# History encoder for 512 users: adding the mask term to the scores and laying out the weight sums on GpSimd, and keeping the short-term sum in PSUM

## What is computed

```python
decay = jnp.exp(-alpha * hist_age_hours) * maskf
mean_hist = (hist_items * maskf[..., None]).sum(1) / (maskf.sum(1, keepdims=True) + 1e-06)
q = mean_hist @ Wq.T
k = jnp.einsum('btd,ed->bte', hist_items, Wk)
v = jnp.einsum('btd,ed->bte', hist_items, Wv)
scores = jnp.einsum('bd,btd->bt', q, k) * scale + jnp.log(decay + 1e-12)
scores = jnp.where(hist_mask, scores, -jnp.inf)
attn = jax.nn.softmax(scores, axis=-1)
long_term = jnp.einsum('bt,btd->bd', attn, v)
# lk marks the last 5 positions below the user's count of unmasked items
short_term = (hist_items * lk[..., None]).sum(1) / denom
g = jax.nn.sigmoid(ctx @ gate_w.T + gate_b)      # ctx: mean popularity, mean age of those 5
user = g * short_term + (1.0 - g) * long_term
# then a layer norm over the 128 columns
```

## Time and profile before

| | us |
|---|---|
| runs without profile | 206.36, 208.58, 211.24 (median 208.58) |
| the profiled execution | 206.09 |
| its span, first to last instruction | 204.4 |
| TensorE busy | 168.8 (83%) |
| VectorE busy | 174.1 (85%) |
| GpSimd busy | 143.0 (70%) |
| ScalarE busy | 118.8 (58%) |

### The profile page before, as it was taken

One profiled execution on the slowest core, in us unless ns is written; L12 is line 12 of the kernel. 1 busy time (PEld: TensorE's weight loads), 2 busy tenths in 40 slices (PEclk: granted clock), 3 DMA queues, 4 the chain that ended last, 5 costly groups with the idle time before them and its releaser, 6 DMA issues.

```text
span 204.4 us, 6882 instructions
## 1 busy us (share of the span) xinstructions
PE 168.8 (83%) x2005; PEld 102.9 (50%) x2005; DVE 174.1 (85%) x1332; ACT 118.8 (58%) x646; POOL 143.0 (70%) x167
## 2 busy tenths in 40 slices
PE   0172864887999699899999999999999999997890
PEld 0132432444565456565655565656565656564570
DVE  0513989989999999999899999898999998989703
ACT  2002255587767377667676777676677776768410
POOL 3467982488959587777869887769698877486311
PEclk9998555699999999999999999999999999999998
DMA  7949969996888878988988899988888998600000
GB/s 36 303 153 304 257 223 420 418 431 287 311 293 326 325 268 287 339 328 277 333 311 331 345 330 338 321 318 323 311 328 287 386 363 313 246 2 14 0 3 13
DMA packets 15683, 55.19 MB, mean 270 GB/s; under 512 B 10160, under 2 KB 11312, under 8 KB 11568
## 3 DMA queue, kind: packets, MB, share of 16 engines
q1 hardware_dynamic: 15088, 53.64, 74.2%
q0 software_dynamic: 576, 1.33, 2.2%
HBM read 54.70 MB, written 0.26 MB: 269 GB/s over the span
## 4 chain that ended last, share of the span: by engine, by line
POOL 31%; issue 25%; PE 17%; DVE 14%; DMA 8%; ACT 3%; POOLq 1%; ACTq 0%; SPq 0%; DVEq 0%
POOL gprod L286 14%; DVE junk_v L686 9%; PE ps_sum L358 6%; POOL mblk L266 6%; DMA x<-in_r_hist_items_dram 5%; POOL pblk L275 5%; PE ps_wx L358 4%; DMA mask_p<-in_r_hist_mask_dram 3%; PE ps_sum L368 3%; PE ps_query L377 2%; POOL pop_taken L344 2%; POOL age_taken L344 2%; ACT sums L467 1%; POOL taken L322 1%; PE ps_group L386 1%
## 5 line engine op out<-in xcount | busy, mean ns | idle before, releaser
L686 DVE SCALAR_TENSOR_TENSOR junk_v<-x,ps_query 128x128 f32<-128x128 f32 x576 | 127.2, 277 | 7.5 <-ACT query L485 7.3
L286 POOL TENSOR_TENSOR gprod<-x,query 128x512 f32<-128x512 f32 x64 | 71.9, 1144 | 32.0 <-ACT query L485 31.9
L458 ACT ACTIVATE gprod<-gprod 128x128 f32<-128x128 f32 x224 | 66.1, 299 | 2.7 <-DVE kept L653 1.4
L358 PE MATMUL ps_wx<-x,pblk 128*32 128x256 f32 (+1 forms) x832 | 67.2, 380 | 0.0
L358 PE MATMUL ps_sum<-x,mblk 128*32 128x256 f32 (+1 forms) x832 | 63.5, 404 | 3.2 <-DMA x<-in_r_hist_items_dram 3.1
L358 PEld LDWEIGHTS ps_sum<-x,mblk 128*32 128x32 f32 (+1 forms) x832 | 34.2, 115 | 25.0 <-issue 7.0
L686 DVE DVE_READ_ACCUMULATOR junk_v<-x,ps_query 128x1 f32 x576 | 45.9, 80 | 0.0
L458 ACT ACTIVATION_READ_ACCUMULATOR gprod<-gprod 128x1 f32 x224 | 42.7, 190 | 0.0
L467 ACT ACTIVATE sums<-ps_sum,rcnt_rows 128x256 f32<-128x256 f32 x32 | 15.1, 472 | 29.9 <-PE ps_sum L358 29.9
L275 POOL TENSOR_TENSOR pblk<-own,ex 128x400 f32<-128x400 f32 x32 | 27.4, 875 | 6.1 <-ACT ex L493 6.1
L358 PEld LDWEIGHTS ps_wx<-x,pblk 128*32 128x32 f32 (+1 forms) x832 | 25.0, 107 | 12.6
(11 more groups left out here) (94 smaller groups left out, 100.4 us busy)
## 6 DMA issues: line engine op xcount, KB each, us to landing
x<-in_r_hist_items_dram SPq DMA_DIRECT2D x32, 1600.0 KB, 8.8
age_p<-in_r_hist_age_hours_dram SPq DMA_DIRECT2D x1, 400.0 KB, 14.6
out_dram<-y SPq DMA_DIRECT2D x4, 64.0 KB, 4.2
mask_p<-in_r_hist_mask_dram SPq DMA_DIRECT2D x1, 100.0 KB, 6.1
mask_u<-in_r_hist_mask_dram SPq DMA_DIRECT2D x1, 100.0 KB, 3.5
wq<-in_L_rec_Wq_dram SPq DMA_DIRECT2D x1, 64.0 KB, 5.7
wk<-in_L_rec_Wk_dram SPq DMA_DIRECT2D x1, 64.0 KB, 3.8
wv<-in_L_rec_Wv_dram SPq DMA_DIRECT2D x1, 64.0 KB, 3.7
```

What stands on the lines that cost most here:

```text
L286: nc.gpsimd.tensor_tensor(gprod[:, t, a * D:b * D].rearrange("p (r d) -> p r d", d=D), rows((k % GP) * PAIR + t, r0 + a, r0 + b), query[:, ...
L358: ins = nc.tensor.matmul(dst[c:c + n * TU, 0:n * D], blk[:, k % 2, t, 2 * m:2 * m + n, :].rearrange("p r u -> p (r u)"), x[:, i + t, 2 * m ...
L458: ins = nc.scalar.activation(src, src, ACT.Copy, accum_out=score[:, k % 2, t, DOTS + r:DOTS + r + 1])
L686: ins = V.scalar_tensor_tensor(out=junk_v[:, t, r, :], in0=x[:, (k % GP) * PAIR + t, r * D:(r + 1) * D], scalar=1.0, in1=c_query[t], op0=A ...
```

## The change

The addition of the mask term moves from VectorE to GpSimd, between `pblk` and the products of tile 0. There it waits for what it waited for before, and in the first step for the mask term itself (`hide_ready`). The four instructions of the maximum stand two dots earlier. The layout of the weight sums moves to GpSimd too, behind the products of tile 0 in step k = 1. The short-term sum is held in a free part of a PSUM bank until its last term, which writes `short` in SBUF as before; the matmul of the denominators, which writes to the same bank, waits for it.

```diff
+        short_sum = ps_fin[:, 384:512]
...
+            def mask_scores(s, k):
+
+                pool.wait_ge(gsums_done, s * PAIR + PAIR)
+                pool.wait_ge(dots_done, s * PAIR + PAIR)
+                if has(s, 1):
+                    pool.wait_ge(exp_done, s * PAIR)
+                else:
+                    pool.wait_ge(hide_ready, 1)
+                nc.gpsimd.tensor_tensor(kept[:, :, 0:ROWS], score[:, k % 2, :, :],
+                                        hide[:, bass.ds(s * PROWS, PROWS)].rearrange("p (t r) -> p t r", t=PAIR),
+                                        ALU.add).then_inc(kept_ready, 1)
+
+            def lay_out_sums(s):
+
+                pool.wait_ge(exp_done, (s - 1) * PAIR)
+                nc.gpsimd.tensor_tensor(wsum_blk[:, :, :], own[:, :].unsqueeze(1).broadcast_to([P, GP * PAIR, TU]),
+                                        wsum[:, :].unsqueeze(2).broadcast_to([P, GP * PAIR, TU]), ALU.mult
+                                        ).then_inc(wsum_ready, 1)
...
                 if has(s, 2):
                     build_pblk(s - 2, k - 2)
+                if has(s, 1):
+                    mask_scores(s - 1, k - 1)
                 if has(s, 0):
                     products(s, k, 0)
+                if k == 1 and has(g, 1, NGROUP):
+                    lay_out_sums(s)
...
                         pe.wait_ge(wsum_ready, g)
+                        pe.wait_ge(short_part, g * LAST)
...
-                link(V.tensor_tensor(hide[:, :], hide[:, :], decay[:, :], ALU.add))
+                V.tensor_tensor(hide[:, :], hide[:, :], decay[:, :], ALU.add).then_inc(hide_ready, 1)
...
-                    ins = V.tensor_scalar(short[:, :], taken[:, i, :], w, None, ALU.mult)
+                    ins = V.tensor_scalar(short_sum, taken[:, i, :], w, None, ALU.mult)
                 else:
                     dve.wait_ge(short_part, g * LAST + i)
-                    ins = V.scalar_tensor_tensor(out=short[:, :], in0=taken[:, i, :], scalar=w, in1=short[:, :],
-                                                 op0=ALU.mult, op1=ALU.add)
+                    ins = V.scalar_tensor_tensor(out=short_sum if i < LAST - 1 else short[:, :], in0=taken[:, i, :], scalar=w,
+                                                 in1=short_sum, op0=ALU.mult, op1=ALU.add)
...
-            def mask_scores(s, k):
-
-                dve.wait_ge(gsums_done, s * PAIR + PAIR)
-                dve.wait_ge(dots_done, s * PAIR + PAIR)
-                if has(s, 1):
-                    dve.wait_ge(exp_done, s * PAIR)
-                V.tensor_tensor(kept[:, :, 0:ROWS], score[:, k % 2, :, :],
-                                hide[:, bass.ds(s * PROWS, PROWS)].rearrange("p (t r) -> p t r", t=PAIR), ALU.add).then_inc(kept_ready, 1)
...
-            def lay_out_sums(s):
-
-                dve.wait_ge(exp_done, (s - 1) * PAIR)
...
-                    if i == DOTS - 2 and k == 1 and fin:
-                        lay_out_sums(s)
...
-                        if i == KEPT_AT:
-                            mask_scores(s - 1, k - 1)
-                        if i == KEPT_AT + 2:
+                        if i == MAX_AT:
                             partition_max(s - 1)
-                        if i == KEPT_AT + 4:
+                        if i == MAX_AT + 2:
                             turn_max(s - 1)
-                        if i == KEPT_AT + 6:
+                        if i == MAX_AT + 4:
                             user_max(s - 1)
-                        if i == KEPT_AT + 8:
+                        if i == MAX_AT + 6:
                             turn_user_max(s - 1)
```

More of the change, by code:

```diff
@@ L49 @@
 MEAN_AT = 2 * D
-KEPT_AT = 9
+MAX_AT = 9
 BIG, FLOOR, TINY = 3.0e38, -1.0e38, 1e-12
@@ L161, in build @@
             sem("sp_exp_in"), sem("sp_exp"), sem("sp_ln_in"), sem("sp_ln"), sem("alpha_ready"), sem("decay_exp"))
-        decay_floored, decay_ln = sem("decay_floored"), sem("decay_ln")
+        decay_floored, decay_ln, hide_ready = sem("decay_floored"), sem("decay_ln"), sem("hide_ready")
         gate_in, gate_exp, rows_ready = sem("gate_in"), sem("gate_exp"), sem("rows_ready")
@@ L673, in turn_user_max @@
                             numax[:, :].unsqueeze(2).broadcast_to([P, Q32 // PU, PU])).then_inc(nmax_ready, 1)
-            def lay_out_sums(s):
-                dve.wait_ge(exp_done, (s - 1) * PAIR)
-                V.tensor_tensor(wsum_blk[:, :, :], own[:, :].unsqueeze(1).broadcast_to([P, GP * PAIR, TU]),
-                                wsum[:, :].unsqueeze(2).broadcast_to([P, GP * PAIR, TU]), ALU.mult
-                                ).then_inc(wsum_ready, 1)
             def dots(s, k, t, a, b):
```

## The result

The changed kernel takes 226.6 us (median of four runs, 223.47 to 227.23) against 207.62 us for the kernel before beside it (206.36 to 211.24). The ratio is 1.089, 95% interval 1.071 to 1.106: clearly slower, and far outside the range of 203.8 to 209.8 us. The profiled execution took 227.23 us, span 225.4.

The account below looks back on a forecast made before the run. TensorE was taken to bound the steady stretch. The 2.02 us wait goes, 0.9 to 1.7 us come back; net gain taken as 0.7 us, so 207.5 - 0.7 = 206.8 us, range 203.8 to 209.8.

Parts of the forecast that it names:

- All this costs nothing: Steady steps: slack such as ScalarE's 0.94 us covers the later addition, layout, maxima and new TensorE wait, at no cost.
- the dear addition: Rival, chance 0.06: the addition on GpSimd takes 1.28 us, each of 14 steps loses 0.45 us, giving 213.8 us.
- TensorE as the bound of the steady stretch: From 84 to 180 us TensorE bounds; sparing VectorE only lengthens its own 3.6 us of waits for queries.
- VectorE is the bound after all: Rival, chance 0.06: VectorE, busy 91.94 of 96 us, bounds the steady stretch, so relieving it gives 194.8 us.
- The wait at 71.32 us: TensorE's 2.02 us wait for VectorE's dots before the query matmul at 71.32 us goes; the most to win.
- The prices: Moved instructions: short terms near 0.35 us each with a PSUM operand, addition 0.30 us, layout 0.45 us on GpSimd.
- GpSimd's queue: Addition ahead of GpSimd's products delays TensorE in two places before 71.32 us, 0.9 to 1.7 us in all.
- the 0.3 us that were forecast: GpSimd's product of 47.03 us starts 0.3 us later behind the addition, and so does TensorE's query matmul at 49.29.
- The wait of 1.5 to 2.5 us for dots in front of the addition near 56 us: Sign of being right: GpSimd waits this long for VectorE's dots before the addition, with the mean copy behind late.
- the forecast 59.0 to 59.7: When ScalarE starts the row sums that it started at 57.05 us, after GpSimd's wait, addition and product.
- 60.0 to 60.8 and 70.2 to 71.0: When TensorE reaches the query matmuls of 59.12 and 71.32 us, 0.9 to 1.7 us late.
- GpSimd's queue gives the gain back: Rival, chance 0.20: dots start no earlier (0 to 0.3 us slower), or the addition takes 0.85 us (207.9 us).

Follow-up runs that it names:

- experiment 1: The changed kernel with eight one-column memsets ahead of VectorE's first instruction, nothing else different: 208.2 us, ratio 1.002.
- experiment 3: The kernel before with only the mask-term addition moved to GpSimd; short-term sum in SBUF, layout on VectorE: 226.1 us, ratio 1.095.
- experiment 7: The kernel before with only the mask-term addition on GpSimd, plus eight memsets ahead on VectorE: 214.6 us, ratio 1.017.
- experiment 8: The kernel before with only the short-term sum moved to PSUM; addition and layout left on VectorE: 205.7 us, ratio 0.994.
- experiment 9: The changed kernel with 128 memsets ahead of VectorE's first instruction: 225.4 us, ratio 1.080.
- experiment 12: Second measurement of the kernel before with PSUM sum and layout on GpSimd, addition left on VectorE: 205.0 us, ratio 0.991.
- experiment 4: The kernel before with the short-term sum in PSUM and the layout on GpSimd, addition left on VectorE: 205.1 us, ratio 0.990.

## Why the prediction was wrong, and where it was right

**The step that failed** is the one on the steady steps that ends in "All this costs nothing". It priced what the instructions do, wait for and hold up, and never what they are: code. The three additions and four semaphore waits that leave VectorE ahead of its loop move the loop across the edge between a fast and a slow place, and that is the whole of the 19 us (experiment 1 takes 18 of them back with eight idle instructions). No term, no rival and no bound of the range held it. The rival on the slower side, the dear addition, named the right instruction and the wrong mechanism: the addition takes 0.29 us, not 1.28. The page before did not show the cost, but it showed the risk: a hardware loop on VectorE, an instruction queue, and no packet on it from 96.5 to 180 us. The changed kernel has six packets between 97 and 160 us. A count of the instructions ahead of it would have shown that seven go; where the boundary lies only the trace of a stalled kernel shows, but that it might be crossed was a rival to name.

**TensorE as the bound of the steady stretch: right.** In experiment 1 VectorE is busy 83.79 us there instead of 91.94, its waits for queries grow from 3.6 to 10.9 us, and TensorE's stay at 2.4. Eight us of relief bought nothing there. The rival "VectorE is the bound after all" (194.8 us) falls.

**The wait at 71.32 us: right.** No TensorE wait for a dot is left in the changed kernel or in any variant with the PSUM sum. It is gone in experiments 3 and 7 too, with the short-term sum still in SBUF.

**The prices: right.** Short terms 0.35 us, the first term's new form included, which had no row (0.34 us); addition 0.29 us (0.30 taken); layout 0.40 us (0.45 taken). No run shows the 0.85 us, twice VectorE's 425 ns, that a rival gave the addition: its mean is 291 ns.

**GpSimd's queue: a loss of about the forecast size, by another mechanism.** With 24 memsets the start looks so, on TensorE, then GpSimd, then ScalarE:

```profile
49.66 0.49 PE L402 MATMUL ps_query<-wqk,mean_p 128*128 128x128 f32 x2 [1.36 <-ACT mean_p L504]
...
51.34 2.66 PE L383 MATMUL ps_sum<-x,mblk 128*32 128x256 f32 x22
...
55.79 0.49 PE L402 MATMUL ps_query<-wqk,mean_p 128*128 128x128 f32 x2
...
61.17 0.49 PE L402 MATMUL ps_query<-wqk,mean_p 128*128 128x128 f32 x2
...
71.20 0.49 PE L402 MATMUL ps_query<-wqk,mean_p 128*128 128x128 f32 x2
```

```profile
55.98 1.70 POOL L277 TENSOR_TENSOR pblk<-own,ex 128x400 f32<-128x400 f32 x2 [1.56 <-ACT ex L519]
57.90 0.29 POOL L301 TENSOR_TENSOR kept<-score,hide 128x50 f32<-128x50 f32 x1 [0.23 <-ACT gprod L484]
58.15 2.23 POOL L288 TENSOR_TENSOR gprod<-x,query 128x512 f32<-128x512 f32 x2
```

```profile
54.15 0.47 ACT L493 ACTIVATE sums<-ps_sum,rcnt_rows 128x256 f32<-128x256 f32 x1 [2.18 <-PE ps_sum L383]
...
59.52 0.31 ACT L484 ACTIVATE gprod<-gprod 128x128 f32<-128x128 f32 x1 [0.44 <-POOL gprod L288]
...
60.71 0.28 ACT L504 ACTIVATE mean_p<-ps_sum 128x128 f32<-128x128 f32 x1 [0.50 <-PE ps_sum L393]
```

and TensorE in experiment 8, which has the same PSUM sum but the addition on VectorE, and whose first query matmul of this stretch starts within 0.25 us of the same time (44.18 and 44.43 us):

```profile
49.17 0.49 PE L378 MATMUL ps_query<-wqk,mean_p 128*128 128x128 f32 x2 [1.12 <-ACT mean_p L480]
...
50.27 1.57 PE L359 MATMUL ps_sum<-x,mblk 128*32 128x256 f32 x22
...
53.62 0.49 PE L378 MATMUL ps_query<-wqk,mean_p 128*128 128x128 f32 x2
...
69.10 0.49 PE L378 MATMUL ps_query<-wqk,mean_p 128*128 128x128 f32 x2
```

The matmul at 49.66 waits 1.36 us instead of the 1.11 of the earlier trace rows, the 0.3 us that were forecast. What the forecast lacked comes behind it: TensorE's granted clock, 1.00 from 44 to 50 us, is 0.50 from 50.2 to 53.5 us, so the next query matmul comes 6.13 us later instead of 4.45. That is 1.68 us, more than the wait itself. The variants with 36, 48 and 136 memsets show the same wait (1.35 or 1.36 us) and a clock of 0.50 from 50 to 52 us; the kernel before and experiment 8, with 1.11 and 1.12 us, stay at 1.00. But experiments 3 and 9 have the wait of 1.36 us too, at 48.90 and 50.07 us, and stay at 1.00, with the next query matmul 4.45 us later. So the longer wait alone doesn't bring the lower clock, and what else it takes isn't shown. With 8 memsets the granted clock was 0.50 up to 50 us anyway; in the changed kernel's trace the query matmul of 47.01 us takes 0.79 us instead of 0.49, though the clock is given as 1.00 from 36 to 50 us. No run varied this wait alone.

The wait of 1.5 to 2.5 us for dots in front of the addition near 56 us did not come here (experiment 7 has it): the addition waits 0.23 us, for ScalarE's row sum. Before it the attention blocks wait 1.56 us for exponentials, and ScalarE is late with those because it waited 2.18 us for TensorE's slowed sums. ScalarE starts at 59.52, within the forecast 59.0 to 59.7 (the step from the product's start at 58.15 to there takes 1.37 us, as from 55.68 to 57.05 in the earlier trace rows; the forecast's sum had 1.2 for it). But then the mean copy waits for TensorE, not TensorE for it: the query matmuls at 61.17 and 71.20 come without a wait, just past the forecast 60.0 to 60.8 and 70.2 to 71.0, because TensorE is late by itself.

**The net.** Without the code stall the four variants give 1.002, 0.994, 0.999 and 1.005, mean 1.000; the forecast was 206.8 / 207.5, or 0.997. That is the forecast to within what the runs tell, or the first reading of the rival "GpSimd's queue gives the gain back" (207.5 to 207.9). That the number fits is partly luck: the wait of 2.02 us went and about 2 us came back, the most of it while the clock was lower (in the trace with 24 memsets) and not in the two places that the prediction added up. Left without the addition, the PSUM sum and the layout win 1%, a little over 2 us and near the 2.02 us that the wait promised, and the addition gives it back.

**Where the addition loses them is shown for about half.** Experiment 8 is at its query matmul of 69.10 us when the kernel with 24 memsets is at 71.20: 2.1 us, of which 0.25 us stand at the start, 0.24 us are the longer wait and 1.68 us the stretch with the granted clock of 0.50 behind it. Some of it is won back by the next loop steps: at the matmuls of 151.39 and 152.70 us the distance is 1.3 us, and the two spans differ by 1.2 us (203.8 and 205.0). In the steady stretch TensorE is as busy with the addition on GpSimd as without it (93.57 us with 24 memsets, 93.69 in experiment 12), and the slack it uses is seen in ScalarE's wait for the mean, 6.5 us in nine pieces instead of the 8.5 of the earlier trace rows. Against experiment 12 the distance is 0.7 us at the matmuls of 81.12 and 80.41 us, though that execution came to its matmul of 46.16 us 1.7 us later than the one with 24 memsets to its own (44.43). The other 1.6 us of the difference of these two spans (205.0 and 202.7) arise in the tail: the granted clock from 190 to 193.4 us is 0.51 with 24 memsets and 1.00 in experiment 12. That isn't the addition's doing, since the clock is below 1.00 there in the profiled executions of experiments 4 and 8 as well (0.62 and 0.67). The medians are 2.3 us apart, and how much of this each place has over many executions stays open.

## What to carry to other kernels

Before pricing an edit to an engine that runs a hardware loop, count the instructions ahead of the loop and in it (accumulator reads and separate semaphore waits included), and ask whether its place can have changed as here, where seven instructions fewer ahead of it cost 19 us; look in the page for instruction packets at the turns of the loop and for idle time put down to issue. If a large loss has no cause in the rows of the work, shift the code by a few idle instructions where the engine waits anyway: that one run tells a cost of the code's place from a cost of the change. And judge the parts of a change only at places where the code lies well, or the verdict is about the place: here the same addition stood at 1.095 and at 1.017. When a change makes TensorE wait a little longer in a place where it already waits, look at the granted clock behind that place, too: here 0.25 us more of waiting were followed by 1.6 to 1.7 us lost at a granted clock near 0.50 in four traces, and by no loss in two.

## What the runs showed of the hardware

- The packets on the instruction queue q14 are of 8 KB (0.17 MB / 21). In all nine traces without a wait of VectorE for issue at the turns of its loop, q14 has no packet between 99 and 160 us; in the five with the wait it has six to eight.
- The place of VectorE's loop decided which it was. The changed kernel was slow as it stood (ratio 1.089), with 48 memsets (1.045) and with 128 (1.080), and fast with 8, 24, 36 and 136 (1.002, 1.005, 0.994, 0.999); the kernel before was slow with 40 (1.044). A shift by 128 instructions brought the same two holes back. That the loop, 344 to 357 instructions long, then touches four pieces of 128 instead of three is a count that fits all of these.
- The waits at a turn hold VectorE for 2.3 to 5.4 us each, and two can stand in a row: in the changed kernel, with 128 memsets and in experiment 3 the second is 4.1 to 5.4 us long; with 48 memsets, and in the kernel before with 40, there is one of 3.7 to 4.0 us.
- A us that VectorE stood cost 1.3 us of time in the changed kernel and with 48 memsets, though TensorE was the bound of the stretch. In the changed kernel TensorE idles for most of it (13.6 us of 15.1), and behind the first gap its granted clock is 0.52 from 121 to 126 us.
- After a wait of TensorE of 1.35 or 1.36 us ahead of the query matmul near 49 us its granted clock was 0.50 from 50.5 to 52 us in four traces (24, 36, 48 and 136 memsets) and 1.00 in two (experiments 3 and 9); after 1.11 and 1.12 us it was 1.00 (two traces).
- The six small setup instructions on VectorE ran beside GpSimd's work in the kernel before and took 0.71 to 0.94 us each there, but for one with 0.18 us. In the changed kernel five of them, from 52.47 us on, fell in GpSimd's wait of 1.72 us and took 0.16 to 0.18 us, and the sixth, as GpSimd began again, 1.30 us; with 8 memsets four did so, and the other two took 1.23 and 0.94 us. The prediction had one to three of them in that wait.
